# One maximum over both PSUM banks of an attention unit's scores, in a two-layer decoder on one core

## The reference

```python
x = x + attn0(layernorm(x))       # 16 heads of 16, causal
x = x + longconv(layernorm(x))    # Toeplitz convolution over the sequence, gated by ctx
x = x + moe0(layernorm(x))        # 2 shared and 16 routed experts
x = x + attn1(layernorm(x))       # 16 heads of 16, causal
x = x + xattn(layernorm(x), ctx)  # 32 heads of 8 over 8 key heads, masked
x = x + moe1(layernorm(x))        # 32 experts with a capacity, and a shared one
```

```python
scores = q @ k.T * s; scores = where(masked, -inf, scores)
p = softmax(scores, axis=-1)
out = p @ v
```

## Time and profile before

| what | value |
|---|---|
| device time, median of 3 | 599.21 us (597.23, 599.21, 603.03) |
| span of the profiled execution | 602.5 us |
| PE busy | 560.4 us, 93% of the span |
| DVE busy | 363.9 us, 60% |
| POOL busy | 306.1 us, 51% |
| mean granted TensorE clock | 0.966 |

### The profile page before, as it was taken

One profiled execution on the slowest core, in us unless ns is written; L12 is line 12 of the kernel. 1 busy time (PEld: TensorE's weight loads), 2 busy tenths in 40 slices (PEclk: granted clock), 3 DMA queues, 4 the chain that ended last, 5 costly groups with the idle time before them and its releaser, 6 DMA issues. The chain is left out here.

```text
span 602.5 us, 12935 instructions
## 1 busy us (share of the span) xinstructions
PE 560.4 (93%) x4865; PEld 343.4 (57%) x4865; DVE 363.9 (60%) x793; ACT 258.8 (43%) x529; POOL 306.1 (51%) x384
## 2 busy tenths in 40 slices
PE   5989997999699999999998799989999997999998
PEld 3545665444446666664665456655555554465587
DVE  5346764899836545452486667776577754872241
ACT  1215453000475666552445245645465553204440
POOL 3418762888765445330034478869799962300000
PEclk8899999999879999998999879999999997999999
DMA  6897009000006333321305991011120031017311
GB/s 216 140 116 287 3 15 414 19 0 0 1 2 189 113 106 102 101 100 45 106 14 69 121 266 46 4 26 35 37 82 2 2 120 41 0 52 299 126 42 62
DMA packets 25133, 53.04 MB, mean 88 GB/s; under 512 B 3515, under 2 KB 16333, under 8 KB 23153
## 3 DMA queue, kind: packets, MB, share of 16 engines
q1 hardware_dynamic: 24357, 51.01, 31.2%
q10 hardware_dynamic: 716, 1.21, 0.6%
HBM read 41.51 MB, written 1.12 MB: 71 GB/s over the span
## 5 line engine op out<-in xcount | busy, mean ns | idle before, releaser
L1314 PE MATMUL PS<-R 128*128 128x256 f16 (+5 forms) x1864 | 203.1, 277 | 2.3 <-DVE R L1178 1.4
L1314 PEld LDWEIGHTS PS<-R 128*128 128x128 f16 (+4 forms) x1864 | 127.7, 104 | 79.3 <-issue 47.7
L796 ACT ACTIVATE R<-PS 128x512 f32<-128x512 f32 x128 | 69.4, 594 | 88.9 <-PE PS L1314 88.8
L1093 DVE TENSOR_REDUCE mx<-PS 128x4 bf16<-128x512 f32 x128 | 82.3, 685 | 34.9 <-PE PS L1314 27.1
L591 POOL TENSOR_TENSOR R<-mx,causal 128x512 bf16<-128x512 bf16 x64 | 66.8, 1064 | 44.1 <-DVE mx L1093 29.8
L1314 PE MATMUL PS<-xnT,R 128*128 128x512 f16 (+1 forms) x348 | 87.1, 392 | 2.1 <-ACT xnT L710 2.1
L591 POOL TENSOR_TENSOR R<-mx,R 128x512 bf16<-128x512 bf16 x64 | 65.4, 1042 | 10.6 <-PE PS L1314 7.0
L1169 DVE TENSOR_TENSOR R<-R,wr 128x512 f32<-128x512 f32 (+1 forms) x46 | 33.8, 734 | 58.9 <-ACT R L874 53.8
L874 ACT ACTIVATE R<-PS,small 128x512 f32<-128x512 f32 (+1 forms) x50 | 34.3, 685 | 51.0 <-PE PS L1314 51.0
L1314 PEld LDWEIGHTS PS<-xnT,R 128*128 128x128 f16 (+1 forms) x348 | 34.6, 101 | 36.6 <-issue 4.7
L539 POOL TENSOR_SCALAR veps<-mv 128x1 f32<-128x1 f32 (+1 forms) x30 | 7.1, 237 | 70.1 <-DVE mv L958 70.0
(11 more groups left out here) (205 smaller groups left out, 797.8 us busy)
## 6 DMA issues: line engine op xcount, KB each, us to landing
R<-in_experts_dram SPq DMA_DIRECT2D x5, 1536.0 KB, 8.3
R<-R SPq DMA_DIRECT2D x48, 128.0 KB, 6.3
wr<-g_scr SPq DMA_DIRECT2D x16, 256.0 KB, 3.3
R<-in_w_dram SPq DMA_DIRECT2D x1, 3200.0 KB, 18.4
R<-in_w_dram SPq DMA_DIRECT2D x1, 3168.0 KB, 11.1
WT<-in_wt_a_dram SPq DMA_DIRECT2D x2, 1024.0 KB, 12.3
R<-in_toe_dram SPq DMA_DIRECT2D x1, 2048.0 KB, 11.4
wr<-g_scr SPq DMA_DIRECT2D x10, 192.0 KB, 2.8
```

The costliest lines, as they stand in the source:

```text
L796: s.activation(PTm[:, n % 4, 4 * k:4 * k + 4, :], bank(2 + (2 * n + k) % 3).rearrange("p (h q) -> p h q", h=4), ACT.Exp, scale=c["sc"]).th ...
L1093: v.tensor_reduce(mx[:, n % 4, 4 * k:4 * k + 4], bank(k).rearrange("p (h k) -> p h k", h=4), AX.X, ALU.max).then_inc(S("att_mx"), 1)
L1314: return nc.tensor.matmul(o_, l, r, start=start, stop=stop)
```

## The change

The two reduces of a unit become one. It reads both banks as 8 heads of 128 keys and writes all eight maxima, and raises `att_mx` by two at its end. The loop over `k` in POOL's stream, the masks on PE and every wait stay as they are; both values that a unit gives to `att_mx` now come at once.

```diff
--- before.py
+++ after.py
@@ -1089,9 +1089,8 @@
                         dve.wait_ge(S("att_s"), n + 1)
                         if n >= 4:
                             dve.wait_ge(S("att_lm"), 2 * (n - 3))
-                        for k in range(2):
-                            v.tensor_reduce(mx[:, n % 4, 4 * k:4 * k + 4], bank(k).rearrange("p (h k) -> p h k", h=4),
-                                            AX.X, ALU.max).then_inc(S("att_mx"), 1)
+                        v.tensor_reduce(mx[:, n % 4, :], PS[:, 0:2, :].rearrange("p a (h k) -> p (a h) k", h=4),
+                                        AX.X, ALU.max).then_inc(S("att_mx"), 2)
                     if done:
                         dve.wait_ge(S("x_updated"), stage * B + b + 1)
                         variance(b)
```

## The result

| | before | after |
|---|---|---|
| median of 15 runs each, in turns | 599.89 us | 605.91 us |
| lowest and highest | 595.78, 605.16 | 600.67, 610.84 |
| after / before | | 1.0111 [1.0086, 1.0136] |
| the profiled execution, and its span | 603.03, 602.5 | 600.95, 599.2 |

A forecast was written before the change was run, and what follows sets the result against it. TensorE (busy 93%) was taken as the bound, VectorE's savings as worth nothing by themselves; 0.52 + 0.45 + 0.5 + 0.91 + 0.53 = 2.9 us, added to the median 599.21, gave 602.1 us, range 597.8 to 606.8.

The forecast's parts named there:

- The reduce: On VectorE, each unit's merged reduce takes 1.22 us against the pair's 1.29, 0.07 less.
- The two releases: After the reduce's start: bank 1 released at 1.22, not 1.29; bank 0 and GpSimd's first half at 1.22, not 0.69.
- A held pair: Where TensorE waits for the maximum, the second mask starts at 1.48 instead of 1.35, 0.13 us later.
- First and second attention: Held masks in their early units and one at 357.94 cost 0.52 us in the first, 0.45 in the second.
- Opening of the third attention: GpSimd is late there, so its 0.53 later start passes through nearly whole to the next queries' normalisation: 0.5 us.
- Its later units: Third attention, seven units with reduces from 418.28 to 479.29, each a held pair: 7 x 0.13 = 0.91 us.
- Elsewhere GpSimd's later start is covered: Outside the third attention's opening and end, GpSimd's 0.53 delay costs nothing; first opening has 1.2 us of slack.
- The end: Third attention's last subtraction starts later and the chain runs through it: the full 0.53 us.
- The sum: Whole kernel: 0.52 + 0.45 + 0.5 + 0.91 + 0.53 = 2.9 us slower.
- rival 2: First attention's first five units: one more idle stretch lowers the clock, 3.3 us on top, 605.4 us; chance 0.12.
- half clock before 52 us: Sign: a clock of 0.5 before 52 us would prove wrong the step that assumed otherwise.
- Rivals 1, 3 and 4: 1: all absorbed, 599.2 us, 0.17; 3: GpSimd bounds third attention, 606.3 us, 0.05; 4: VectorE paced more, 594.7 us, 0.03.

The follow-up runs named there:

- after_mid: The changed kernel with GpSimd's rstd computed between the two subtractions of a unit instead of behind both; 603.70 us, ratio to before 1.0058.
- after_again: The changed kernel once more, unaltered, timed beside later experiments; 606.32 us, ratio to before 1.0103.
- pe_late: The kernel before, two reduces kept, with only TensorE's first mask made to wait for both maxima; 603.95 us, ratio to before 1.0046.
- pool_late: The kernel before, two reduces kept, with only GpSimd's first half made to wait for both maxima; 601.89 us, ratio to before 1.0014.
- after_fill: The changed kernel with five unread matmuls ahead of the masks in steps 1 to 3 of the first two attentions; 601.65 us, ratio to before 1.0029.
- cross_only: The kernel before with the single reduce in the third (cross) attention alone, the pair kept elsewhere; 602.12 us, ratio to before 1.0015.
- before_mid: The kernel before with GpSimd's rstd computed between the two subtractions of a unit instead of behind both; 597.81 us, ratio to before 0.9964.

## Why the prediction was right or wrong

**The reduce, right.** 1.222 us against 1.22. Starting from the reduce's own row and adding the slope was better than the estimate by the Trainium skill ("Perfetto Trace Analysis", section "Optimizing Scalar/DVE Operations"), 1.17 us. The same section's rule on breaking instructions up pointed the right way.

**The two releases, right.** First mask at 1.28, GpSimd 1.37 to 1.40 after the reduce's start; 1.28 and 1.4 forecast.

**A held pair, undersized.** 0.13 forecast, 0.19 in the openings at full clock and 0.21 in the steady cycle once `rstd` is out of the way (`after_mid`). I took the start of the second mask, 1.48 in place of 1.35, with the masks 0.20 apart. The pair takes 0.61, not 0.59, a lone mask 0.39, and the second one starts 0.22 to 0.23 behind the first, at 1.51: that makes 0.16. The last 0.03 arise between the second mask and the next reduce, and I can't place them.

**First and second attention, undersized by a third.** 0.52 and 0.45 forecast, 0.79 and 0.72 measured at full clock (the second 0.64 with 10.2 us of half clock on both sides). In the first, four pairs at 0.19 make 0.76.

**Opening of the third attention, right in size.** 0.5 forecast, and 0.13 for the held pair at 418.28 that lies in it; 0.58 measured (`after_again`, 24.13 against 23.55). TensorE's masks alone make 0.21 of it (`pe_late`, 23.76), so GpSimd's share is about 0.4.

**Its later units: two steps failed.** Six of the sum's seven held pairs lie here, 0.78. From the ninth unit to the last it is 1.94 (65.17 against 63.23), 1.16 more.
- *The price of a held pair.* `after_mid`, where `xn` doesn't wait in the steady cycle, has 0.20 to 0.21 at each of the six places, about 1.25 where the sum had 0.78.
- *"Elsewhere GpSimd's later start is covered".* I had worked that out for one of GpSimd's two customers, TensorE, which wants the subtraction two units later, and only in the first opening. The other one, `rstd`, stands behind the subtraction in GpSimd's queue, `xn` waits for it, and the next reduce stands behind `xn`. The earlier trace rows showed this very chain, but I took it for a matter of the opening. `pool_late` shows it alone, 0.76 over these units (63.99). On top of the held masks it adds 0.34 (64.83 in `after_mid`, 65.17 in after).
- *One unit.* The twelfth takes 3.09 us from reduce to reduce where before's takes 2.74. It does so in `after_mid` and `after_fill` too, but in neither `pool_late` nor `pe_late`. No run shows what makes these 0.35.

**The end, right.** 0.53 forecast; from the last reduce to the last `xn` 15.39 against 14.87, and 15.40 or 15.41 in `after_again`, `after_fill` and `cross_only`.

**The sum.** Fixed cost: 0.79 + 0.72 + 2.52 + 0.52 = 4.6 us, where I had 2.9. The times at the same clock agree, 4.1 to 4.4 us, and so does the timed pair with the filling: 1.0029 - 0.9945 = 0.84%, 5.0 us (by the two intervals 2.8 to 7.3).

**The clock, rival 2: a part of it.** The whole change costs 6.7 us (5.2 to 8.2 by its interval), 4 to 5 of them at an equal clock. The lower granted clock of the changed kernel's runs makes about 1.4 us more by the fit. The forecast's sum had this term at nothing, since TensorE was busy for only 1.53 of 3.00 us with the clock at 1.00; one of its signs of being wrong, half clock before 52 us, came true. Rival 2 named the first opening and a price of 3.3; the profiles show 3.4 to 6.8 us at half clock there. But its condition, that one more idle stretch decides, isn't shown: `pool_late`, `cross_only` and `before_mid` had half clock in the first opening with masks that wait as before. Why the changed kernel meets the lower clock more, and how the 1.4 us are shared out over the program, stays open.

**Rivals 1, 3 and 4 fell.** The loss isn't absorbed. GpSimd isn't the bound: at 483.97 and 487.02 it still waits 0.28 and 1.02 us for a maximum, although its lateness costs. The 8.0 us that VectorE was spared bought nothing. (That rival 3's 606.3 us lies near the result is chance.)

## What to carry to other kernels

Merging two instructions on an engine with time to spare saves its overhead, here 0.07 us of 1.29, and delays the first result by half the work, here 0.53: count who waits for that first result. Price a held instruction by the time to the next round of the loop, not by its own start: here 0.19 to 0.21 where 0.13 was reckoned, and held masks are more than half of the fixed cost. Follow the lateness through every in-order queue that it enters, not only to the data's own reader: here a one-column instruction behind the late one held VectorE and the next reduce. Compare times at the same granted clock before reading a difference of one percent. And where TensorE waits about a microsecond at a time while a stage opens, try giving it something to do: five short matmuls in each of six such gaps brought this kernel from 598.36 to 596.14.

## What the runs showed of the hardware that was not expected

*VectorE's normalisation stands still until GpSimd's instruction is over.* `xn`, one instruction of 256 f32 elements, takes 0.41 us where GpSimd does nothing, and 1.12 beside its subtraction in after. The end of after, timeline, with GpSimd idle at 489.94 (its `rstd` ends at 489.90):

```profile
485.63 1.23 DVE L1092 TENSOR_REDUCE mx<-PS 128x8 bf16<-128x1024 f32 x1 [0.40 <-PE PS L1313]
...
487.02 2.04 POOL L591 TENSOR_TENSOR R<-mx,R 128x512 bf16<-128x512 bf16 x2 [1.02 <-DVE mx L1092]
...
489.94 0.41 DVE L972 TENSOR_SCALAR xn<-X,mv,rstd 128x256 f32<-128x256 f32 x1 [2.54 <-POOL rstd L540]
```

GpSimd's queue in the steady cycle, timeline of after:

```profile
445.10 2.08 POOL L591 TENSOR_TENSOR R<-mx,R 128x512 bf16<-128x512 bf16 x2
```

of before:

```profile
447.55 2.08 POOL L591 TENSOR_TENSOR R<-mx,R 128x512 bf16<-128x512 bf16 x2
```

and of `after_mid`:

```profile
448.39 3.08 POOL L592 TENSOR_TENSOR R<-mx,R 128x512 bf16<-128x512 bf16 x3
```

A half of the subtraction takes 1.04. In after it ends at 446.14 and `xn` at 446.29; in before at 448.59 and 448.73; in `after_mid` at 449.42 and 449.58. In these three `xn` is over 0.14 to 0.16 after the half that ran when it started, whenever it started. By that the 0.94 of before and the 1.12 of after are mostly waiting: released by `rstd`, `xn` now starts at the very beginning of the next half and waits for all of it. It can be worse. In the second attention of before one `xn` started while GpSimd was 0.11 from the end of one instruction and 0.07 from the start of the next, and ended 0.15 after that next one:

```profile
376.94 1.26 DVE L972 TENSOR_SCALAR xn<-X,mv,rstd 128x256 f32<-128x256 f32 x1
```

The statistics of the same data (`stats`, one input as well) and the reduce, which reads PSUM, are not held: 0.42 and 1.22 to 1.23 beside GpSimd as without it. The Trainium skill, in "SBUF — State Buffer", says that VectorE and GpSimd share a pair of ports as an exclusive lock that one of them holds for a whole instruction, and that only some of VectorE's forms take it; `xn` agrees, and GpSimd shows the other side of it: the half that begins as a held `xn` ends takes 1.09 in place of 1.04 (446.10 in after). The port wasn't tried apart.

*The granted clock varies with nothing changed.* The same instructions of the first opening ran at 1.00 in the profile of before and at 0.51 in that of `cross_only`. That five matmuls of 256 columns in a gap would keep it at 1.00 was a guess; it held in the first two openings of all four profiles that have them. The third attention has none, and there `after_fill` has 3.4 us at half clock.
